# Depooling and low-rank experts: the normalisation moves from VectorE to ScalarE, with scale and bias made on GpSimd

## The reference, cut to what matters

```python
x = x + _L0_xattn_ref(_layernorm(x, axis=-1), ctx_2048, mask_BxS2_if0, ...)
...
x = x + _L3_xattn_ref(_layernorm(x, axis=-1), ctx_2048, mask_BxS2_if0, ...)
...
x = x + _L3_ffn_ref(_layernorm(x, axis=-1), ...)

# depooling
h = rmsnorm(embeds, g_res)
h = jnp.einsum('bld,ed->ble', h, W_in) + b_in
h_patch = rmsnorm(patch_embeds, g_init)
return _hnet_depool(h, h_patch, patch_lens)      # a decaying sum of the patches, picked by row, plus h

# low-rank experts
logits = x @ gate_w.T
scores = jax.nn.softmax(logits, axis=-1)
weights, idx = jax.lax.top_k(scores, TOP_K)      # 2 of 8
base = x @ W_lin.T + b_lin
t = jnp.einsum('nd,nkdr->nkr', x, left[idx])     # rank 4
out_k = jnp.einsum('nkr,nkro->nko', t, right[idx])
return base + jnp.sum(weights[..., None] * out_k, axis=1)
```

## Time and profile before

| | us |
|---|---|
| median of 3 runs | 3903.31 |
| lowest and highest | 3892.40 and 3909.63 |
| the profiled execution, whole | 3910.36 |
| its span, from the first to the last instruction | 3908.2 |

### The profile page before, as it was taken

The page is one execution under the profiler, slowest core; times in us unless marked ns, Lnnn a source line. Parts: engine busy times, 40 slices in busy tenths (PEclk is TensorE's granted clock), DMA queues, the critical chain, the costliest instruction groups (busy, mean ns, idle before and its releaser), DMA issues. The chain is left out here.

```text
span 3908.2 us, 106170 instructions
## 1 busy us (share of the span) xinstructions
PE 3360.9 (86%) x39854; PEld 2856.4 (73%) x39856; DVE 2672.6 (68%) x7741; ACT 1648.2 (42%) x4070; POOL 1231.1 (31%) x1704
## 2 busy tenths in 40 slices
PE   3787899999968888797899999999999999874756
PEld 2675788888846666545689999999999999743345
DVE  7774899999948888667355555555555555469776
ACT  1231677777727777564122222222222222223342
POOL 3552788888713333303100000000000000145042
PEclk8897999999979999898699999999999999968677
DMA  3000000000012222200275565556555565355000
GB/s 92 4 0 36 1 0 0 0 0 0 1 42 77 76 75 75 58 1 7 45 134 125 121 125 115 125 124 126 125 114 125 125 127 124 64 100 78 1 3 24
DMA packets 374617, 253.41 MB, mean 65 GB/s; under 512 B 118452, under 2 KB 371336, under 8 KB 373672
## 3 DMA queue, kind: packets, MB, share of 16 engines
q1 hardware_dynamic: 369960, 244.92, 28.9%
q10 hardware_dynamic: 4352, 4.20, 0.5%
HBM read 233.01 MB, written 15.75 MB: 64 GB/s over the span
## 5 line engine op out<-in xcount | busy, mean ns | idle before, releaser
L2146 ACT ACTIVATE L_xattn_prob<-psum,L_xattn_nmax 128x258 f32<-128x258 f32 x512 | 239.2, 472 | 958.4 <-DVE L_xattn_nmax L2178 958.4
L933 PE MATMUL psum<-L_ffn_share,L_ffn_prob 128*128 128x128 f32 x4096 | 495.0, 278 | 54.7 <-DVE L_ffn_prob L866 54.7
L2267 PE MATMUL psum<-L_xattn_ctxT,L_xattn_q_ctx 128*128 128x257 f32 x2048 | 523.2, 388 | 9.0 <-issue 4.7
L933 PEld LDWEIGHTS psum<-L_ffn_share,L_ffn_prob 128*128 128x128 f32 x4096 | 472.1, 193 | 73.8 <-DVE L_ffn_prob L866 58.8
L751 POOL TENSOR_TENSOR L_ffn_sums<-L_ffn_sims 128x1024 f32<-128x1024 f32 x256 | 486.6, 1913 | 106.7 <-DVE L_ffn_prob L866 106.7
L2289 PEld LDWEIGHTS psum<-L_xattn_probT,L_xattn_ctx 32*128 32x128 f32 x16384 | 471.1, 187 | 47.0 <-DVE L_xattn_q_ctx L2169 41.0
L2289 PE MATMUL psum<-L_xattn_probT,L_xattn_ctx 32*128 32x128 f32 x16384 | 496.0, 274 | 4.0 <-DVE L_xattn_probT L2192 2.1
L2122 POOL TENSOR_TENSOR L_xattn_z_var<-L_xattn_z_mv,L_xattn_z_eps 128x1 f32<-128x1 f32 x32 | 6.1, 191 | 1328.8 <-DVE L_xattn_z_mv L2204 1295.8
L2267 PEld LDWEIGHTS psum<-L_xattn_ctxT,L_xattn_q_ctx 128*128 128x128 f32 x2048 | 362.0, 191 | 58.0 <-DMA L_xattn_ctx<-ctx_dram 4.8
L790 ACT ACTIVATE psum<-L_ffn_sums,L_ffn_bias 128x512 f32<-128x512 f32 x512 | 340.4, 688 | 94.1 <-DVE L_ffn_prob L866 89.9
L866 DVE SCALAR_TENSOR_TENSOR L_ffn_prob<-L_ffn_sums,L_ffn_best,psum 128x512 f32<-128x512 f32 x512 | 357.8, 740 | 5.7 <-ACT psum L790 2.4
(11 more groups left out here) (439 smaller groups left out, 6149.5 us busy)
## 6 DMA issues: line engine op xcount, KB each, us to landing
L_xattn_ctx<-ctx_dram SPq DMA_DIRECT2D x512, 256.0 KB, 5.4
L_xattn_ctxT<-ctx_T_dram SPq DMA_DIRECT2D x128, 257.0 KB, 3.1
L_xattn_k_all<-ctx_T_dram SPq DMA_DIRECT2D x128, 128.5 KB, 2.1
L_xattn_v_all<-ctx_dram SPq DMA_DIRECT2D x128, 128.0 KB, 2.3
L_attn_qkv_scratch<-L_attn_qkv SPq DMA_DIRECT2D x24, 256.0 KB, 2.8
L_attn_rows<-L_attn_qkv_scratch SPq DMA_DIRECT2D x24, 256.0 KB, 5.2
start_raw<-ctx_dram ACTq DMA_DIRECT2D x16, 256.0 KB, 12.3
start_plug_all<-plug_scratch SPq DMA_DIRECT2D x1, 2048.0 KB, 7.1
```

What stands on the lines that cost most here:

```text
L933: last = nc.tensor.matmul(pair(2 * s)[:, c * P:(c + 1) * P], prob[:, h % RING, c * P:(c + 1) * P], share[:, h % RING, :], start=(h == 0 an ...
L2146: ins = nc.scalar.activation(prob[:, s, g, :], scores(s)[:, g, :], ACT.Exp, bias=nmax[:, s, g:g + 1], accum_out=total[:, s, g:g + 1])
L2267: last = nc.tensor.matmul(scores(s)[:, g, 0:CTX], q_ctx[:, p, c, b, h:h + 4, :].rearrange("p h n -> p (h n)"), ctxT[:, b, c, :], start=(c ...
```

## The change

In the three layers the normalised tiles are written by ScalarE: an activation with the function Identity, the scale rstd and the bias -mean*rstd, both one number per row. GpSimd makes the bias with two added operations behind each block of factors (a multiplication, and a multiplication by -1), each behind a wait for its pipeline, and counts it in `centred`. In depooling, the bias addition b_in moves from GpSimd to VectorE and waits there for `normed`, VectorE takes the moments one pair earlier, and `add(g-1)` follows `add_bias(g)`. In the experts' layer the bias addition stays on GpSimd; new waits for `normed` stand ahead of the moments on VectorE and ahead of the factors on GpSimd, since `mv` and `rstd` of that buffer are now read by another engine.

```diff
@@ depool_cross, GpSimd
-            front.pool_rstd(pool, 0, only=tiles(0))
-            front.pool_rstd(pool, 0, only=tiles(1))
+            def normal_factors(r):
+                front.pool_rstd(pool, 0, only=r)
+                lo, hi = r[0], r[-1] + 1
+                pool.drain()
+                nc.gpsimd.tensor_tensor(shifted[:, lo:hi, 0:1], front.mv[:, lo:hi, 0:1], front.rstd[:, lo:hi, :], ALU.mult)
+                pool.drain()
+                nc.gpsimd.tensor_scalar(shifted[:, lo:hi, 1:2], shifted[:, lo:hi, 0:1], -1.0, None,
+                                        ALU.mult).then_inc(centred, len(r))
+
+            normal_factors(tiles(0))
+            normal_factors(tiles(1))
             pool.wait_ge(rows_in, 32)
             patches(0)
             patches(1)
             for g in range(2, GROUPS, 2):
-                front.pool_rstd(pool, 0, only=pair(g))
-                add_bias(g - 2)
+                normal_factors(pair(g))
                 patches(g)
-                add_bias(g - 1)
                 patches(g + 1)
-            add_bias(GROUPS - 2)
-            add_bias(GROUPS - 1)
@@ depool_cross, ScalarE
+            def normalise(g):
+                act.wait_ge(centred, (g + 1) * S)
+                for t in tiles(g):
+                    nc.scalar.activation(front.xn[:, t, :], core.x[:, t, :], ACT.Identity, bias=shifted[:, t, 1:2],
+                                         scale=front.rstd[:, t, :]).then_inc(front.normed, 1)
+
+            normalise(0)
             for g in range(GROUPS):
+                if g + 1 < GROUPS:
+                    normalise(g + 1)
                 act.wait_ge(front.turned, (g + 1) * S)
@@ depool_cross, VectorE
+            def add_bias(g):
+                dve.wait_ge(front.normed, (g + 1) * S)
+                nc.vector.tensor_tensor(x_of(g), x_of(g), over(b_in), ALU.add)
+
             def add(g):
                 dve.wait_ge(out_done, g + 1)
-                dve.wait_ge(biased, g + 1)
+                dve.drain()
                 nc.vector.tensor_tensor(x_of(g), x_of(g), out_bank(g), ALU.add).then_inc(added, 1)
...
-            for g in range(1, GROUPS + 2):
-                if g % 2 and g + 2 < GROUPS:
-                    front.dve_moments(dve, 0, only=pair(g + 1))
-                if g < GROUPS:
-                    front.dve_normalise(dve, 0, only=tiles(g))
-                if g >= 2:
-                    add(g - 2)
+            front.dve_moments(dve, 0, only=pair(2))
+            dve.wait_ge(rows_in, 32)
+            for g in range(GROUPS):
+                if g % 2 and g + 3 < GROUPS:
+                    front.dve_moments(dve, 0, only=pair(g + 3))
+                add_bias(g)
+                if g >= 1:
+                    add(g - 1)
+            add(GROUPS - 1)
@@ lora_experts, GpSimd
                 if live(-2):
-                    front.pool_rstd(pool, g * S + 2 * S - v * S, only=slots(v))
+                    pool.wait_ge(front.normed, (g + 1) * S)
+                    normal_factors(g + 2, v)
@@ lora_experts, ScalarE
+            def normalise(g, v, waits):
+                act.wait_ge(centred, g + 1)
+                if waits:
+                    act.wait_ge(front.turned, (g - 1) * S)
+                for s in slots(v):
+                    nc.scalar.activation(front.xn[:, s, :], core.x[:, g * S + s - v * S, :], ACT.Identity,
+                                         bias=shifted_mean[:, s, 1:2], scale=front.rstd[:, s, :]).then_inc(front.normed, 1)
...
                 if live(0):
                     exp(g)
+                if live(0) and live(-2):
+                    normalise(g + 2, v, True)
@@ lora_experts, VectorE
                 if live(-2):
+                    dve.wait_ge(front.normed, (g + 1) * S)
                     moments(g + 2, v)
                 if live(0):
                     weigh(g, v)
-                if live(-2):
-                    normalise(g + 2, v, True)
```

35 lines of the change are left out of this document (19 added, 16 removed).

## The result

The changed kernel takes 3871.9 us in the median of six runs (3851.9 to 3878.8), the kernel before 3899.8 us, also in six runs, three of them those of the table before (3892.4 to 3909.6). The ratio is 0.9918, with a 95% interval of 0.9903 to 0.9934: 27.9 us less by the medians, faster by more than 0.5%. The forecast was 3876.5 us, with a range of 3862 to 3896.

What follows compares the result with a forecast made beforehand. VectorE was taken as the bound, its depooling normalisation stretched by GpSimd's bias and patch operations. Two depooling stages at 10.4 us plus 6 in the experts' layer gave 26.8 off 3903.3, so 3876.5 us, range 3862 to 3896.

Steps and rivals of the forecast that it cites:

- the new chain: Depooling stages: GpSimd's factors and patches set the pace, the last factors ending at 25.6 us; 10.4 us saved per stage.
- the middle: Depooling stage end at 35.9 us, taken between 34.5 and 37.3 for GpSimd waiting on VectorE's bias addition.
- no delay: Depooling: GpSimd loses nothing when it meets VectorE's bias addition; the last addition ends at 34.5 us.
- every delay: Depooling: at most four bias additions delay GpSimd's chain by 0.69 us each, 2.8 in all; the stage ends at 37.3.
- a waiting addition hides on VectorE: Depooling: each of 8 bias additions may wait up to 1.27 us for a patch, hidden by VectorE's spare 10.97-5.1.
- The rival in which the factors cost what the power costs: Depooling and experts: each added GpSimd operation takes 1.64 us; total 3906 to 3910 us or more; chance 0.02.
- the longer tile: Rival: ScalarE's four tiles cost 1.69 us instead of 1.08, giving +14.6 over 24 groups and 3918 us; chance 0.01.
- the rise: Depooling: TensorE's clock goes from low to high near 22 us of the stage, after gapless work from about 16.6.
- The rival that the clock stays low: TensorE at low clock replaces VectorE as the bound; only 5 to 15 us saved, 3888 to 3898; chance 0.23.
- the slow value of the loop: Experts' layer: the two-step loop through GpSimd, ScalarE, TensorE and VectorE takes 13.2 us, 6.6 a step, at low clock.
- the band of 5.7 to 6.8 that I had given as a sign: Experts' layer: steps of 5.7 to 6.8 us, with narrowT copied right after a normalisation, would show the forecast right.
- at most 0.2 a step: Experts' layer: cost in us where a small two-input VectorE operation meets GpSimd's bias addition, counted inside the bounds.

Runs made afterwards that it cites:

- e11_filler: Six extra TensorE transposes of the identity a step in the experts' layer, against the changed kernel; 2.4 us less than the changed kernel, in one profile.

## Why the prediction was right, step by step

**The depooling chain.** I had named GpSimd's factors as the new chain and worked out where each block ends. Measured ends, in us of the stage, beside the forecast without any meeting: 7.4 (7.3), 13.7 (13.4), 20.3 (19.5), 27.0 (25.6). The last block is 1.4 us late: 3 x 0.45 us for GpSimd's first operation beside VectorE's addition, 0.32 on one power and 0.25 on one issue, less a pair that is otherwise 0.2 shorter than I had it. From there to the last addition I had put 8.9 us; it took 9.1. That the middle that I took between "no delay" (34.5) and "every delay" (37.3), 35.9, came within 0.2 of the measured 36.1 is partly luck. A meeting comes in each of the three pairs (I had allowed for four in a stage), and costs 0.45 instead of 0.69; the power and the issue that lost 0.57 in all I had not counted, nor the pair's 0.2 that go the other way. By the reading that I had given of the Trainium skill's section, the full 0.69 for each of four meetings, the stage would have taken 37.3: the blocking is real, the price was too high by a third. The kernel with the bias in PSUM measured the lower bound itself, 34.1 and 34.5.

One reason of mine was wrong without harm. That a waiting addition hides on VectorE I had read from 10.97-5.1 us to spare, but the new pair is 6.6 us long, not 10.97. From the last moments at 82.83 on, VectorE was busy 6.03 of 6.57 us, and these moments ended 0.57 us before GpSimd asked for them. The waiting was hidden by half a microsecond, not by six.

**The prices.** Two added GpSimd operations: 0.8 forecast, 0.77 from the power's end to theirs in a pair (1.02 where one issue took 0.41), and 0.72 by the kernel with two more. Four tiles on ScalarE: 1.7 forecast, 1.65. GpSimd's pair: 6.1 forecast; 6.3 to 6.7 with the meetings, 5.9 without them in the kernel with the bias in PSUM (6.1 once, with one issue of 0.41). The rival in which the factors cost what the power costs is thereby out, and so is the longer tile: ScalarE waits 15 us for factors in the first stage.

**The clock.** Here the sum was right and its path was not quite. I had the rise near 22 us of the stage. It came for a moment at 16, went, and came for good at 20.2; from there the window is at 0.99:

```profile
74.00:83.00 9.00, 7.69 (x38) 6.71 (x38) 2.83 (x4) 4.13 (x10) 7.64 (x11) 0.69 0.00 0
83.20:99.20 16.00, 13.76 (x111) 12.47 (x109) 10.30 (x26) 8.86 (x21) 8.53 (x11) 0.99 0.01 2
```

Over the whole stage it is 0.76, not above 0.8 as I had asked (0.82 in the second). The rival that the clock stays low would have left the stage at 45.6 (by its own terms 45.8 at the least, from 16.6 with seven times 3.4 and six times 0.9); its milder form exists. The first stage of the kernel with two more operations and both stages of the kernel with the gates first had a relapse, and paid 1.6 and 1.7 us each (the second stage of `e11_filler` took 37.8 us too). I had treated the clock as all or nothing, with 0.23 for the bad case; what the runs show is a toll of about 1.7 us a relapse in the last pair.

**The experts' layer.** The forecast was 6 us and 6.2 were measured, but by other pieces. First logits at 10.0, measured 9.8; second at 15.0, measured 14.7. The third came at 22.3 instead of 23.4, since the first long step took 7.6 and not 8.4: 1.0 us gained that I had not counted. The next four steps took 5.5, 7.6, 5.8 and 7.5, 6.6 in the mean, where I had taken 6.2: the slow value of the loop. Against the 7.7 that I had put for each step of before they would have given 4.5 us and not 6. They gave 5.6, because the last of the four took 8.67 in the kernel before, a length that I had not read. The step after them lost 0.4. So 6 was met with luck: four steps each too slow by 0.4, and the 0.4 lost after them, were paid for by two gains outside my sum, 1.0 and 1.1. The loop's slow value of 6.6 a step was right as a mean (its terms as listed add up to 13.0 for two steps, not 13.2); that its two steps would not be alike, and that the low clock would hold in just the long ones, I had not seen, and neither 5.5 nor 7.6 lies in the band of 5.7 to 6.8 that I had given as a sign. The small VectorE operations beside GpSimd's bias addition were under-priced, "at most 0.2 a step": the subtraction L3179, of two SBUF tiles, took 1.04 and 0.78 instead of 0.19 in two steps of the changed kernel,

```profile
3829.49 1.04 DVE L3179 TENSOR_TENSOR L_ffn_gate<-L_ffn_gate,L_ffn_best 128x32 f32<-128x32 f32 x1
...
3863.45 0.78 DVE L3179 TENSOR_TENSOR L_ffn_gate<-L_ffn_gate,L_ffn_best 128x32 f32<-128x32 f32 x1
```

and the two of the kernel with the gates first lost 2.1 us together. Of the two rows shown the first stands in the first long step, ahead of the moments that GpSimd waits for, and the second in the step that lost 0.4.

**The time.** The forecast was 3903.3 less 26.8, 3876.5; the median is 3871.9. Of the 4.6 us between them 3.5 are the kernel before, which came out at 3899.8 this time. The changed stages gave 26.8 and the medians give 27.9; runs that scatter by 9 us don't tell these two apart.
